# Transposing the gating rows of a GPS layer: seven of ten tiles by way of DRAM quarters and VectorE instead of TensorE

## What is computed

```python
xn = layernorm(x)
x  = x + gnn(xn, W, a, src, dst) + mix(xn, w_ql, w_qr, w_key, w_value)
x  = x + ffn(layernorm(x), gate_W, gate_b, expert_W, expert_b)
# gnn: h = xn @ W;  e = exp(-leaky_relu(al[src] + ar[dst]));  elu(segment_sum(e * h[dst]) / segment_sum(e))
# ffn: scores = max(xn2 @ gate_W + gate_b, EPS); top 2 of 8 experts for each node; weighted sum of their outputs
```

## Time and profile before

| | us |
|---|---|
| median of 3 runs | 1188.06 (1186.6 to 1189.08) |
| the profiled execution, its time | 1190.13 |
| the profiled execution, its span | 1188.3 |
| TensorE busy | 1134.6 (95%) |
| VectorE busy | 628.7 (53%) |
| ScalarE busy | 309.0 (26%) |
| GpSimd busy | 524.2 (44%) |
| mean granted TensorE clock | 0.978 of full speed |

### The profile page before, as it was taken

How to read it: one execution, slowest core, us unless ns; L and a number is a source line. 1 busy time by engine, 2 the same in 40 slices (tenths; PEclk the granted TensorE clock), 3 DMA queues, 4 the chain that set the end, 5 groups by cost and what they waited for, 6 DMA issues and landing times.

```text
span 1188.3 us, 15303 instructions
## 1 busy us (share of the span) xinstructions
PE 1134.6 (95%) x5408; PEld 971.2 (82%) x5408; DVE 628.7 (53%) x1411; ACT 309.0 (26%) x418; POOL 524.2 (44%) x397
## 2 busy tenths in 40 slices
PE   6999999999999999999999999999968899999995
PEld 5798888888788999999988878888856688778774
DVE  7935766555332122211133447997579753765555
ACT  2421212133111121211022213343354311523232
POOL 0003557457687477711000015233315566575655
PEclk9999999999999999999999999999958899999998
DMA  9382875773533544477457633463277965886753
GB/s 353 110 353 45 234 198 115 242 205 36 138 47 43 93 93 93 98 158 154 91 177 242 198 117 115 166 242 131 95 283 284 338 110 100 249 240 134 186 93 71
DMA packets 117099, 192.14 MB, mean 162 GB/s; under 512 B 35224, under 2 KB 65176, under 8 KB 115888
## 3 DMA queue, kind: packets, MB, share of 16 engines
q1 hardware_dynamic: 81120, 159.53, 39.1%
q0 software_dynamic: 35920, 31.83, 19.9%
HBM read 136.19 MB, written 61.68 MB: 167 GB/s over the span
## 4 chain that ended last, share of the span: by engine, by line
PE 83%; DVE 10%; DMA 3%; issue 2%; POOL 1%; ACT 1%; DVEq 0%; POOLq 0%; ACTq 0%
PE ps L1615 26%; PE ps L1616 26%; PE ps L1617 26%; DVE e_lo L1418 3%; DMA out<-y,row_put 2%; PE ps L1763 2%; PE ps L1703 2%; DVE xn_lo L1141 1%; DVE stats L1113 1%; DVE acc L1129 1%; DVE ps L1521 1%; PE ps L1661 1%; DMA out_seen<-out 1%; POOL gx L827 0%; DMA acc<-in_x 0%
## 5 line engine op out<-in xcount | busy, mean ns | idle before, releaser
L749 POOL DMA_INDIRECT cnt_d<-times,addr_i x160 | 265.9, 1662 | 181.3 <-DMA cnt_d<-times,addr_i 97.1
L1615 PE MATMUL ps<-e_hi,lt_hi 128*128 128x512 f32 x368 | 147.8, 402 | 16.8 <-DVE yb L1589 10.9
L1616 PE MATMUL ps<-e_lo,lt_hi 128*128 128x512 f32 x368 | 145.4, 395 | 0.0
L1617 PE MATMUL ps<-e_hi,lt_lo 128*128 128x512 f32 x368 | 145.0, 394 | 0.0
L1616 PE MATMUL ps<-xt_lo,q_hi 128*128 128x416 f32 (+1 forms) x384 | 135.0, 352 | 0.0
L1615 PE MATMUL ps<-xt_hi,q_hi 128*128 128x416 f32 (+1 forms) x384 | 135.0, 352 | 0.0
L1617 PE MATMUL ps<-xt_hi,q_lo 128*128 128x416 f32 (+1 forms) x384 | 134.7, 351 | 0.0
L827 POOL DMA_INDIRECT gx<-xn_d,tok_now x92 | 93.1, 1012 | 68.3 <-DVE tok_now L1584 36.0
L1615 PEld LDWEIGHTS ps<-e_hi,lt_hi 128*128 128x128 f32 x368 | 70.3, 191 | 38.9 <-DVE yb L1589 13.2
L860 POOL DMA_INDIRECT out<-y,row_put x46 | 78.0, 1695 | 37.7 <-DVE y L1575 18.1
L1282 DVE TENSOR_TENSOR qs<-ps,qs 128x416 f32<-128x416 f32 (+1 forms) x24 | 14.2, 592 | 135.6 <-PE ps L1617 135.6
(11 more groups left out here) (267 smaller groups left out, 2382.8 us busy)
## 6 DMA issues: line engine op xcount, KB each, us to landing
e_raw<-in_L_ffn_expert_W SPq DMA_DIRECT2D x64, 512.0 KB, 8.8
cnt_d<-zeros SPq DMA_DIRECT2D x20, 640.0 KB, 12.3
rows<-key_d SPq DMA_DIRECT2D x8, 1250.0 KB, 7.2
acc<-in_x SPq DMA_DIRECT2D x18, 512.0 KB, 7.4
w_raw<-in_L_mix_w_key SPq DMA_DIRECT2D x16, 512.0 KB, 4.3
cnt_d<-cnt_d POOLq DMA_DIRECT2D x10, 640.0 KB, 7.7
cnt<-cnt_d SPq DMA_DIRECT2D x10, 640.0 KB, 6.0
h_d<-hs SPq DMA_DIRECT2D x18, 256.0 KB, 2.0
```

What stands on the lines that cost most here:

```text
L749: nc.gpsimd.indirect_dma_start(out=cnt_d[i], out_offset=bass.IndirectOffsetOnAxis(ap=addr_i[:, j:j + 1], axis=0), in_=times[:, j:j + 1], i ...
L1615: nc.tensor.matmul(o, lh, rh, start=(k == 0), stop=False)
L1616: nc.tensor.matmul(o, lh, rl, start=False, stop=False)
L1617: return nc.tensor.matmul(o, ll, rh, start=False, stop=(k == last_k))
```

## The change

Tiles 0 to 6 (`TURNED = NT - 3 = 7`) no longer go through TensorE's transposes and ScalarE's copies. Instead SyncE, at the start of its step t, waits until `xn2` of tile t-2 has landed in DRAM and loads it back, a quarter of the columns at a time, into a new buffer `xq`. There partition 32q+j holds, at position t of four, quarter q of row 32t+j. VectorE then turns 32 x 32 blocks of `xq` in one instruction into `xg`, which is the transposed tile in the natural order of features. TensorE's gating product of these tiles takes a second copy of the gating matrix, `gw_nat`, in the natural order. Tiles 7 to 9 go as before. Three semaphores are saved by counting on others further up (`s_pre`, `s_padt`, `s_padp`), with the same producers and the same waiters. The core of the diff, in the order of the file; `load_quarters` runs on SyncE, `gate_in` on ScalarE, `rows_turned` on VectorE, and the last two pieces on TensorE:

```diff
+        TURNED = NT - 3
+        xq = at("xq", R2 + 2 * D, [P, 2, D])
+        gw_nat = at("gw_nat", R3 + KB * NE + 2 * P + NT // 2 * P, [P, KB, NE])
...
-            if 2 <= t < NT - 1:
-                tr_jobs(t - 2)
...
+            def load_quarters(i):
+                sp.wait_ge(s_xn2d[i % 2], 16 * (i // 2 + 1))
+                if i >= 2:
+                    sp.wait_ge(s_xg, i - 1)
+                for q in range(NQD):
+                    sp.dma_start(xq[q * QD:(q + 1) * QD, i % 2, :].rearrange("j (t k) -> j t k", t=NQD),
+                                 xn2_d[i * P:(i + 1) * P, q * QK:(q + 1) * QK].rearrange("(t j) k -> j t k", t=NQD)).then_inc(s_xq[i % 2], 16)
             for t in range(NT + 1):
+                if 2 <= t < TURNED + 2:
+                    load_quarters(t - 2)
                 if t < NT:
...
                 if t == 0:
+                    sp.dma_start(gw_nat[:, :, :], gate_W.rearrange("(k p) e -> p k e", p=P)).then_inc(s_gw, 16)
...
-                if t >= 4:
-                    gate_in(t - 4)
...
+            def rows_turned(i):
+                dve.wait_ge(s_xq[i % 2], 16 * NQD * (i // 2 + 1))
+                if i >= 2:
+                    dve.wait_ge(s_gate_used, i - 1)
+                V.transpose(xg[:, i % 2, :, :].rearrange("p c (t j) -> p c t j", t=NQD),
+                            xq[:, i % 2, :].rearrange("p (t c i) -> p c t i", t=NQD, c=KB)).then_inc(s_xg, 1)
...
                     nc.vector.reciprocal(rs, rs).then_inc(s_rsum, 1)
+                if 3 <= t < TURNED + 3:
+                    rows_turned(t - 3)
                 if t + 1 < NT:
                     scores(t + 1)
...
                     if i >= 2:
-                        dve.wait_ge(s_full, tr_job[i - 2] + 2)
+                        if i - 2 >= TURNED:
+                            dve.wait_ge(s_full, tr_job[i - 2] + 2)
                         dve.wait_ge(s_xn2d[i % 2], 16 * (i // 2))
...
-                pe.wait_ge(*released(tr_job[i] + 1))
+                if i < TURNED:
+                    pe.wait_ge(s_xg, i + 1)
+                else:
+                    pe.wait_ge(*released(tr_job[i] + 1))
+                g_w = gw_nat if i < TURNED else gw
...
                     if t >= 3:
                         gate(t - 3)
-                    if t >= 2:
-                        rows_transposed(t - 2)
```

More of the change, by code:

```diff
@@ L163, in gps_layer @@
         R3 = R2 + 11 * D
+        TURNED = NT - 3
+        xq = at("xq", R2 + 2 * D, [P, 2, D])
         gw = at("gw", R3, [P, KB, NE])
+        gw_nat = at("gw_nat", R3 + KB * NE + 2 * P + NT // 2 * P, [P, KB, NE])
+        assert R3 + 2 * KB * NE + 2 * P + NT // 2 * P <= BIG and ROWS[TURNED - 1] == P
         att_sum = at("att_sum", R3 + KB * NE, [P, 2, P])
@@ L452, in gps_layer @@
         s_turn = sem("s_turn")
+        s_xq, s_xg = [sem(f"s_xq{i}") for i in range(2)], sem("s_xg")
         s_put, s_y, s_sc = sem("s_put"), [sem(f"s_y{h}") for h in range(2)], [sem(f"s_sc{h}") for h in range(2)]
-        s_gpos, s_non, s_nonp, s_pre, s_padt, s_pad, s_padp, s_rows, s_step = (sem(n) for n in (
-            "s_gpos", "s_non", "s_nonp", "s_pre", "s_padt", "s_pad", "s_padp", "s_rows", "s_step"))
+        s_gpos, s_non, s_nonp, s_pad, s_rows, s_step = (sem(n) for n in (
+            "s_gpos", "s_non", "s_nonp", "s_pad", "s_rows", "s_step"))
         s_chain = sem("s_chain")
@@ L832, in _ @@
             pool.wait_ge(s_non, 1)
-            pool.wait_ge(s_pre, 1)
+            pool.wait_ge(s_gexp, 2)
             step(G.tensor_tensor(pad_at[:, :], pad_pre[:, :], pad_0[:, :], ALU.add))
@@ L1048, in _ @@
             act.wait_ge(s_nonp, 1)
-            nc.scalar.copy(pad_pre[:, :], ps[:, 6, 0:NE]).then_inc(s_pre, 1)
+            nc.scalar.copy(pad_pre[:, :], ps[:, 6, 0:NE]).then_inc(s_gexp, 1)
             act.wait_ge(s_bounds, 1)
@@ L1544, in _ @@
             last.then_inc(s_wtab, 1)
-            dve.wait_ge(s_padt, 1)
+            dve.wait_ge(s_non, 2)
             V.tensor_tensor(last_c[:, :, :], io16[:, 0:NSLOT].unsqueeze(1).to_broadcast([P, NE, NSLOT]),
@@ L1553, in _ @@
             expert_lo(0, range(FIRST_LO, KB))
-            dve.wait_ge(s_padp, 1)
+            dve.wait_ge(s_nonp, 2)
             link(V.tensor_tensor(slot_f[:, :], ps[:, 6, 64:64 + NSLOT], slot_f[:, :], ALU.add))
@@ L1759, in gate @@
                 if i == 0:
-                    pe.wait_ge(s_gw, 16 * 2 * NQD + 16)
-                pe.wait_ge(*released(tr_job[i] + 1))
+                    pe.wait_ge(s_gw, 16 * 2 * NQD + 32)
+                if i < TURNED:
[3 more added lines that the diff above has]
+                g_w = gw_nat if i < TURNED else gw
                 for k in range(KB):
-                    last = nc.tensor.matmul(ps[0:w, 7, i * NE:(i + 1) * NE], xg[:, i % 2, k, 0:w], gw[:, k, :],
+                    last = nc.tensor.matmul(ps[0:w, 7, i * NE:(i + 1) * NE], xg[:, i % 2, k, 0:w], g_w[:, k, :],
                                             start=(k == 0), stop=(k == KB - 1))
@@ L1855, in _ @@
                 last = nc.tensor.matmul(ps[:, 6, 64:64 + NSLOT], pad_r[:, e, :], pad_c[:, e, :], start=(e == 0), stop=(e == NE - 1))
-            last.then_inc(s_padp, 1)
+            last.then_inc(s_nonp, 1)
             for e in range(NE):
```

2 lines of the change are left out of this document (1 added, 1 removed).

## The result

The changed kernel takes 1222.96 us, the median of four runs (1221.32 to 1223.62), beside 1187.33 (1185.33 to 1189.08) of the kernel before: **1.0292 times the time, interval 1.028 to 1.0304, 35.6 us slower**. (The ratio is not the quotient of the two medians, which is 1.0300; the difference lies within the spread of the runs.) Its profiled execution took 1222.4 us with a span of 1220.6; before it was 1190.13 and 1188.3, so the two traces lie 32.3 us apart.

The account below looks back on a forecast made before the run. TensorE, 95% busy, was taken as the bound, VectorE some 2 us a pass behind. Seven trips with transposes (57.4), six rests (74.4) and 6.5 us delay pass 9: 33.3 us on 1188.06 gives 1221 us, range 1209 to 1235.

Parts of the forecast that it names:

- Removed and small parts: TensorE's seven times eight transposes gone, 6.5 us if TensorE stays the bound; extra loads, gating matrix and merged semaphores, 0.
- The trip: From finished `xn2` through DRAM write, four load issues and landing to VectorE's transpose: 6.9 us, bounds 6.2 and 9.2.
- The transpose: VectorE's transpose of a tile in `rows_turned`: 1.25 us, 1.3 with its start, bounds 1.2 and 1.8.
- The rest: VectorE's pass from the scores to the next attention split, behind the wait: 12.4 us, as in pass 4.
- shorter-loop rival: VectorE's loop has a trip of 5.5 us and a rest of 10.7; pass 9 13 us late, 1201 us; chance 0.10.
- the sum: From 741.2, seven trips with transposes, six rests and a last 6.5 us; pass 9 ends at 897.1, 33.3 us lost.
- The turn: One pass of VectorE's loop through DRAM: 20.6 us against TensorE's 15.57, making VectorE the bound from pass 4 or 5.
- Tile 7: Its `xn2` ready at 879.5 instead of 842.0, so TensorE waits about 15 us ahead of pass 9.
- The end of pass 9: On TensorE, at 897.1 instead of 863.84, including 2.7 us for a slow start; everything after as before.
- The clock: TensorE may start each pass at half clock after idling, 18.3 us a pass, hidden under VectorE's 20.6.
- The clock that stays down: TensorE at half clock throughout, 28.5 us a pass, is the bound again; 60 us lost, 1248 us; chance 0.05.
- The faster one: Wait in `rows_turned` stays within VectorE's lead, needing a 3.6 us trip; whole 6.5 us gained, 1181.6 us; chance 0.04.

Follow-up runs that it names:

- The run with the loads alone: Kernel before, with the change's seven times four quarter loads issued by SyncE and no other engine waiting for them; 1190.39 us, ratio 1.0007.
- the cut product: Changed kernel, wait and transpose moved into VectorE's idle stretch behind the variance, gating product split into two lots of eight matmuls; 1184.68 us, ratio 0.9947.
- the uncut versions: Changed kernel, gating product whole, wait and transpose moved behind the weights (1189.57 us, again 1188.61) or into VectorE's idle stretch behind the variance (1186.85).
- the version with the wait in the gap: Changed kernel with wait and transpose moved to VectorE's 0.66 us idle stretch behind the variance, gating product whole; 1186.85 us, ratio 0.9977.

## Why the prediction was right

The forecast was 1221 us, slower; the measured 1222.96 is 2 us above it. The mechanism came out as forecast: VectorE's waits for the loads, the spacing of its splits and TensorE's one long wait are all there. That the number is met within 2 us is partly luck, as two misses of opposite sign show below. By its steps:

- **Removed and small parts.** The run with the loads alone bears out the zeros for traffic, issues and merged semaphores. A pass of TensorE without a wait takes 15.65 us (15.57 foretold), so the 6.5 us were some 0.6 too many; with VectorE as the bound that is hidden. The load of `gw_nat` is issued at 711.33 and the counts at 716.70, 0.5 us later than before; pass 3's split is at 741.01 (741.14 before), so that is 0 as taken.
- **The trip, 6.9 us foretold.** VectorE's idle time is 5.5 us on average, and 1.9 lie under split and reciprocal: 7.45. VectorE's waits are 5.0 to 6.1 us where 4 to 5 were named. From the issue of the last quarter to the transpose it is 2.9 to 4.0 us, 3.3 on average, not 2.8; some 0.3 of that is the write of `out`, which the working did not count among the transfers in flight.
- **The transpose, 1.3.** 1.246 us, near the 1.25 of the text, but the working does not give that figure: 0.449 + 768 x 1.218 / 1024 is 1.36. The measured slope between 256 and 1024 columns is (1.246 - 0.449) / 768 = 1.04 ns a column, less than the 1.19 of the operation in the earlier trace rows. The error is 0.1 us a turn.
- **The rest, 12.4.** 12.40 us; GpSimd's sums fell together with VectorE's small step, as in pass 4 of before. So 10.7 of the shorter-loop rival was rightly left aside in the sum.
- **The turn, 20.6.** 21.05 us, six of them.
- **Tile 7.** `xn2` at 882.1 (879.5 foretold), TensorE's wait 15.6 us (about 15), transposes and pass 9 in 899.47 - 882.15 = 17.3 us (17.6). The start at half clock was there, but only in part where it was counted: the eight transposes took 1.97 us for the 0.9 of the sum, and 7 matmuls behind them stood 0.43 us apart, where the sum had 13.
- **The end of pass 9.** 899.5 instead of 897.1: 35.6 us late where 33.3 were foretold. 3.3 us came back later in the profiled execution, which the sum had taken as nothing; it took 1222.4 where the sum had 1223.4. So 2.3 us too few in this part and 3.3 too many behind it nearly cancel: that is the luck. Between the medians the loss is 35.6.
- **The clock.** Half clock after each wait, and hidden. One turn in busy times:

```profile
749.00:765.00 16.00, 16.00 (x81) 13.54 (x81) 14.14 (x18) 3.39 (x4) 4.07 (x5) 1.00 0.27 97
785.00:805.00 20.00, 16.94 (x78) 14.05 (x77) 13.60 (x16) 4.74 (x6) 4.01 (x5) 0.93 0.63 222
...
865.00:880.00 15.00, 1.55 (x14) 1.46 (x14) 9.38 (x15) 2.42 (x4) 2.55 (x5) 0.66 0.41 141
```

TensorE is busy for all of the 16.00 us in its pass 3, before VectorE's loop has used up the lead; in the second row it has 3.06 us idle and the clock is 0.93. The third row lies in the wait for tile 7. The chain has matmuls 0.43 us apart from 785.32 on, behind a wait of 4.3, and 0.23 from 788 on. The Trainium skill, TensorE: Matmul & The Clock Gate, section "HAM oscillation — how this bites in real kernels", has a product that starts slow in each round of a loop that waits; passes 5 to 8 here agree with it, with 0.43 us for 0.23 behind 2.8 to 4.3 us of waiting.

The rivals: the shorter loop falls with the rest of 12.40 and the trip of 7.5. The clock that stays down falls with the recovery 3 to 6 us after each wait (784.5 to 788 in pass 5, 805.8 to 811.9 in pass 6). The faster one named its place rightly, the wait in `rows_turned`: with the same trip and the wait 9 us later in the pass, the change does gain, 0.5 to 0.6% with the cut product. What would decide was not a shorter trip, as the rival had it, but other work ahead of the wait.

What stays open: why the clock falls behind the gating product in the uncut versions (3, 3 and 2 times in passes 4 to 8) and did not in the kernel before, where TensorE's transposes stood behind the same product. It does not fall behind every whole product either: of fifteen such places in three executions eight have a stretch, and the changed kernel has none at its one place without a wait (762.61). With the cut there is none at fifteen places. So the cut prevents it, as three runs show; the reason is not shown. Open too is why a pass without the transposes is 0.85 us shorter and not 0.93; another 0.05 is lost with the cut.

## What to carry to other kernels

When an engine works in order and waits for data that it sent out itself one step earlier, price the loop: trip plus everything between the wait and the next send. Moving the wait behind independent work takes it out of the sum, best to a place where the engine idles anyway. Here two moved lines were worth 3%, while the work that the change took from TensorE was worth 0.5%. And when an engine is unloaded by moving work to one that is nearly as busy, give the work a place under an existing stall, or the second engine sets the pace at once.

## What the runs showed of the hardware that was not expected

- TensorE's granted clock fell to its lower level, 1.2 GHz, without any idle time before, behind sixteen matmuls of 8 columns (1.8 us, fed densely): 8 stretches at fifteen places in three executions whose product was whole, each costing about 1.6 us; none behind the product in three executions that cut it into lots of 0.8 to 0.9 us with a half pass between.
- Loads from DRAM to SBUF landed in 2.0 us at 64 KB and 2.9 at 128 KB (medians of 56 and 28, issue to landing). Cutting the four loads into eight added 1.86 us of issue a tile and made the trip only 0.7 us longer.
- A whole trip through DRAM for 512 KB, from the end of the producing instruction to the start of the consuming one, with four loads issued from one queue, is 7.45 us, of which the issues are 1.8.
- VectorE's operation on one element (`nt`, behind the variance) took 1.52 us in pass 4 of the kernel before, from 766.73 to 768.25, and GpSimd's first sum of 128x640 ran from 766.66 to 768.23. With the transpose ahead of it (the version with the product cut) it began at 752.80 and ended at 753.91, again with that sum (752.33 to 753.89). Where no such sum ran (838.35, the version with the wait in the gap) it took 0.12.
